# Pairs in three GpSimd instructions and six smaller moves in a two-layer gated-attention kernel

## What is computed

```
x = x + tanh(g_xattn[0]) * L0_xattn(ctx, ctx, layernorm(x), ssm_kernel, D, 8)   # (8, 256, 512)
x = x + tanh(g_ffn[0])   * L0_ffn(layernorm(x), w1, w2, w3)      # hidden 1408, ternary weights
x = x + tanh(g_xattn[1]) * L1_xattn(layernorm(x), ctx, mask)     # softmax attention on ctx
x = x + tanh(g_ffn[1])   * L1_ffn(layernorm(x), w1, w2, w3)      # hidden 2048, sign weights
# L0_xattn: kv = einsum('bhil,bhjl->bijhl', k, v); y = causal conv of kv with ssm_kernel + kv * D
#           out = einsum('bijhl,bhil->bjhl', y, q)                # 32 heads of 8
# ffn: h = silu(quant(x) @ W1.T) * (quant(x) @ W2.T); out = quant(h) @ W3.T
#      L0 quantises by row, L1 by groups of 64
```

## Time and profile before

| | us |
|---|---|
| three runs | 699.57, 700.22, 700.86 (median 700.22) |
| profiled execution | 699.74, of which span 697.6 |
| TensorE busy | 685.9 (98% of the span), granted clock 0.999 |
| VectorE / ScalarE / GpSimd busy | 587.8 / 410.1 / 273.4 |

### The profile page before, as it was taken

How to read it: one execution, slowest core, us unless ns; L and a number is a source line. 1 busy time by engine, 2 the same in 40 slices (tenths; PEclk the granted TensorE clock), 3 DMA queues, 4 the chain that set the end, 5 groups by cost and what they waited for, 6 DMA issues and landing times.

```text
span 697.6 us, 9561 instructions
## 1 busy us (share of the span) xinstructions
PE 685.9 (98%) x3172; PEld 389.6 (56%) x3172; DVE 587.8 (84%) x1066; ACT 410.1 (59%) x630; POOL 273.4 (39%) x413
## 2 busy tenths in 40 slices
PE   9999999999999999999999999999999999999997
PEld 8777777777444444567654444444444444444445
DVE  4999899899999998658958999888888888888791
ACT  3688898866579989748577544334434434434340
POOL 5779989987765654537500001111110111110000
PEclk9999999999999999999999999999999999999999
DMA  8887765553369979997040243363332333332244
GB/s 295 278 238 205 205 192 143 152 143 107 96 159 180 198 175 204 216 356 305 17 135 16 61 103 70 83 92 91 75 82 41 75 91 91 77 91 45 61 68 113
DMA packets 155376, 94.64 MB, mean 136 GB/s; under 512 B 133824, under 2 KB 134336, under 8 KB 155328
## 3 DMA queue, kind: packets, MB, share of 16 engines
q1 hardware_dynamic: 153600, 90.02, 50.6%
q0 software_dynamic: 1200, 3.93, 1.7%
q10 hardware_dynamic: 528, 0.09, 0.1%
HBM read 53.04 MB, written 8.47 MB: 88 GB/s over the span
## 4 chain that ended last, share of the span: by engine, by line
PE 73%; DVE 14%; POOL 3%; issue 3%; DMA 3%; ACT 2%; SPq 1%; POOLq 0%; ACTq 0%; DVEq 0%
PE psum L860 26%; PE psum L709 13%; PE psum L892 13%; PE psum L787 7%; PE psum L799 4%; PE psum L843 3%; PE psum L821 3%; DVE phase_space L1234 2%; DVE phase_space L1340 1%; DVE phase_space L1243 1%; DVE psum L1236 1%; DVE ln_bn L280 1%; DVE phase_space L1407 1%; PE psum L876 1%; PE psum L721 1%
## 5 line engine op out<-in xcount | busy, mean ns | idle before, releaser
L860 PE MATMUL psum<-phase_space 128*128 128x512 f16 x1024 | 224.0, 379 | 1.7 <-DMA phase_space<-phase_space 1.6
L860 PEld LDWEIGHTS psum<-phase_space 128*128 128x128 f16 x1024 | 99.9, 98 | 124.1 <-DMA phase_space<-phase_space 2.1
L709 PE MATMUL psum<-phase_space 128*128 128x288 f32 x640 | 159.2, 407 | 2.1 <-DVE phase_space L1243 1.9
L709 PEld LDWEIGHTS psum<-phase_space 128*128 128x128 f32 x640 | 120.0, 190 | 35.3 <-issue 3.2
L688 POOL DMA_DIRECT2D out<-x_sb x15 | 9.3, 620 | 303.9 <-DVE x_sb L1421 303.9
L892 PE MATMUL psum<-phase_space 128*128 128x512 f16 x480 | 105.7, 379 | 0.0
L1181 ACT ACTIVATE phase_space<-psum,b_scalars 128x512 f32<-128x512 f32 x64 | 43.5, 682 | 80.6 <-PE psum L860 78.7
L1187 ACT ACTIVATE phase_space<-phase_space,magic 128x1024 f32<-128x1024 f32 x32 | 36.4, 1147 | 77.2 <-DVE phase_space L1400 77.2
L787 PE MATMUL psum<-phase_space 128*128 128x512 bf16 (+1 forms) x384 | 79.0, 361 | 0.5 <-DVE phase_space L1282 0.5
L892 PEld LDWEIGHTS psum<-phase_space 128*128 128x128 f16 x480 | 46.9, 98 | 56.7
L1385 DVE SCALAR_TENSOR_TENSOR phase_space<-psum,b_scalars,phase_space 128x512 f32<-128x512 f32 x64 | 47.6, 747 | 25.9 <-ACT phase_space L1181 25.9
(11 more groups left out here) (122 smaller groups left out, 1039.1 us busy)
## 6 DMA issues: line engine op xcount, KB each, us to landing
phase_space<-in_L_weights SPq DMA_DIRECT2D x24, 512.0 KB, 5.8
phase_space<-in_L_weights SPq DMA_DIRECT2D x12, 704.0 KB, 7.4
phase_space<-kpad SPq DMA_DIRECT2D x14, 512.0 KB, 4.3
phase_space<-in_context_heads SPq DMA_DIRECT2D x15, 384.0 KB, 5.1
x_sb<-in_x_tiles SPq DMA_DIRECT2D x16, 256.0 KB, 4.8
phase_space<-in_context_turned SPq DMA_DIRECT2D x8, 512.0 KB, 6.1
x_between<-x_sb SPq DMA_DIRECT2D x16, 256.0 KB
x_sb<-x_between SPq DMA_DIRECT2D x16, 256.0 KB, 6.9
```

The source lines that it names most:

```text
L709: return nc.tensor.matmul(at(bank(4 * hh + lo), 0, [[64, B], [1, NP]]), toep[n % 2][:, hh, (lo - li) * P:(lo - li + 1) * P], kv[n % 2][:, ...
L860: last = nc.tensor.matmul(bank(2 * (m % 3) + w), fb_qT[n % 2][:, kk % 2, kk // 2, :], b_wT[w][:, kk // 2, c * 512:(c + 1) * 512], start=(k ...
```

## The change

Seven edits.

1. `pairs(n)` for n >= 1 writes its 24 products in three instructions of 64x8 elements, one for each distance, instead of one of 64x3x8.
2. `warm_up` issues 12 matmuls instead of 17.
3. `a_scale_x(n + 3 - NT)` of steps 13 and 14 comes behind products(n, 1) on VectorE instead of ahead of it.
4. `low_h` of tiles 0, 1 and 2 of the last FFN goes to GpSimd, with b_norm(4) between those of tiles 0 and 1; VectorE keeps tiles 3 to 15.
5. SyncE transposes x of tile 3 ahead of the rows of tile 1, instead of behind them.
6. The x side of tile 15: scale and up scales on VectorE move to the end of tile 13, ahead of fb_product(14, 0); rounding on ScalarE moves one silu ahead, and fb_deq_x ahead of fb_product(14, 1).
7. sign_b(11) moves from ScalarE's last step of the first FFN to step 0 of the attention, and c_stats(15) from step 9 to step 10.

```diff
-        NBA = 12
-        SIGN_STEP = {3: 12, 5: 13, 6: 14, 7: 15, 8: 16, 13: 17, 15: 18}
+        NBA = 11
+        SIGN_STEP = {0: 11, 3: 12, 5: 13, 6: 14, 7: 15, 8: 16, 13: 17, 15: 18}
...
-        C_STEP = {0: (4,), 1: (5,), 2: (6,), 3: (7,), 5: (8,), 6: (9, 10), 7: (11, 12), 8: (13, 14), 9: (15,)}
+        C_STEP = {0: (4,), 1: (5,), 2: (6,), 3: (7,), 5: (8,), 6: (9, 10), 7: (11, 12), 8: (13, 14), 10: (15,)}
...
                 for n in range(NT):
-                    if 2 <= n < NT - 1:
+                    if 3 <= n < NT - 1:
                         fb_turn_x(n + 1)
+                    if n == 1:
+                        fb_turn_x(3)
...
-                    nc.gpsimd.tensor_tensor(at(kv_k, E, [[NP, rows], [E, 3], [1, E]]),
-                                            at(cx_sb[k], 0, [[EX, rows], [0, 3], [1, E]]),
-                                            at(cx_sb[k], 1, [[EX, rows], [1, 3], [1, E]]), ALU.mult)
+                    for d in range(1, 4):
+                        nc.gpsimd.tensor_tensor(at(kv_k, d * E, [[NP, rows], [1, E]]),
+                                                at(cx_sb[k], 0, [[EX, rows], [1, E]]),
+                                                at(cx_sb[k], d, [[EX, rows], [1, E]]), ALU.mult)
...
+                for n in range(3):
+                    if n == 1:
+                        b_norm(4)
+                    for g in range(4):
+                        low_h(pool, nc.gpsimd, n, g)
                 for n in range(NT - 1):
-                    if n + 4 < NT:
+                    if 1 <= n < NT - 4:
                         b_norm(n + 4)
...
-                    for _ in range(17):
+                    for _ in range(12):
...
-                        if (c == 2 and 3 <= n < NT - 2) or (c == 1 and n in (2, NT - 2)):
+                        if (c == 2 and 3 <= n < NT - 2) or (c == 1 and n == 2) or (c == 0 and n == NT - 2):
                             fb_round_x(n + 1)
...
+                    products(n, 1)
                     if NT - 3 <= n < NT - 1:
                         a_scale_x(n + 3 - NT)
-                    products(n, 1)
...
                     if n == NT - 2:
-                        fb_scale_x(n + 1)
-                        fb_up_scales(n + 1)
+                        fb_deq_x(n + 1)
...
-                    for g in range(4):
-                        low_h(n, g)
+                    if n >= 3:
+                        for g in range(4):
+                            low_h(dve, nc.vector, n, g)
+                    if n == NT - 3:
+                        fb_scale_x(NT - 1)
+                        fb_up_scales(NT - 1)
```

More of the change, by code:

```diff
@@ L301, in ln_norm, with low_h @@
                                     ALU.add, ALU.mult).then_inc(s_done, 1)
+        def low_h(eng, ops, n, g):
+            eng.wait_ge(h_hi, n * 4 + g + 1)
+            if n == 3 and g == 0:
+                eng.wait_ge(h_lo, 12)
+            ops.tensor_tensor(fb_tp[n % 2][:, 1, g * 512:(g + 1) * 512], fb_t[n % 2][:, g * 512:(g + 1) * 512],
+                              fb_tp[n % 2][:, 0, g * 512:(g + 1) * 512], ALU.subtract).then_inc(h_lo, 1)
         def spread(row, groups):
@@ L1409, in deq_h @@
                                                    ).then_inc(h_u, 1)
-                def low_h(n, g):
-                    dve.wait_ge(h_hi, n * 4 + g + 1)
-                    nc.vector.tensor_tensor(fb_tp[n % 2][:, 1, g * 512:(g + 1) * 512], fb_t[n % 2][:, g * 512:(g + 1) * 512],
-                                            fb_tp[n % 2][:, 0, g * 512:(g + 1) * 512], ALU.subtract).then_inc(h_lo, 1)
                 def b_residual(n):
@@ L1575, in _ @@
                     fb_product(n, 1)
-                    if n in (2, NT - 2):
+                    if n == 2:
                         fb_deq_x(n + 1)
@@ L1618, in _ @@
                 for g in range(4):
-                    low_h(NT - 1, g)
+                    low_h(dve, nc.vector, NT - 1, g)
                 b_residual(NT - 3)
```

## The result

The changed kernel takes 693.9 us (median of six executions, 692.84 to 695.37), the kernel before 699.93 in the same comparison: a ratio of 0.9913, interval 0.9899 to 0.9926. In two later comparisons it was 692.90 (ratio 0.9899, 0.9886 to 0.9911) and 693.12 (0.9908, 0.9892 to 0.9923). It is faster by 6.0 to 6.9 us, where the forecast was 701.0 and the range ended at 694.0.

The account below looks back on a forecast made before the run. TensorE, busy 685.9 of 697.6 us, bounds the kernel; with pieces GpSimd would pace the conv stage: +3.45 us there, -2.3 behind it, net +1.15 on the profiled 699.74, lying 0.5 below the median: 701.0. Range 694 to 704.

Parts of the forecast that it names:

- Edit 1, the price of a piece: GpSimd, pairs(n): a 64x8 multiply takes 1.27 us, so three pieces add 1.0 us a step; bounds 0 and 1.0.
- The two groups: Earlier GpSimd rows: two different inputs, 2.15 ns an element and 0.18 us fixed; repeated input, 1.64 and 0.23.
- The second group's 1.07: Price in us of a 64x8 piece by the rows with repeated input (L561, L566); three take 3.1.
- The step of GpSimd: Conv stage: bare step 8.8 us, 9.8 with pieces, 10.8 with two folds, against the 10.24 TensorE needs.
- rival C: Conv stage: pieces no dearer per element than L566, step 10.1 us, GpSimd never sets the pace; 694.6 to 695.1; chance 0.33.
- The first four steps: Start of conv stage: pairs(1) ends at 19.2 us and conv(1, 0) waits for it; conv(4, 0) stays at 50.45.
- the head's gain: Edit 2: with five matmuls fewer the first conv starts 1.6 us earlier, which is spent waiting for pairs(1).
- Edit 3: End of conv stage: takes away three TensorE waits for L1243, 0.87 + 0.74 + 0.40 = 2.0 us, if nothing else is late.
- The list of waits: TensorE's waits: conv stage 0.87, 0.74, 0.40 and 0.26 us, all for VectorE; later 0.26, 0.44, 1.05 and 0.52.
- Behind the conv stage: Later waits go: edit 7 takes 0.26 and 0.44 us, edits 4 and 5 1.05, edit 6 0.52; sum -2.3 us.

Follow-up runs that it names:

- gpsimd_load: The changed kernel with one more 128x64x4 product a step on GpSimd, written to a buffer nobody reads: 702.65 us, ratio 1.004 to the kernel before.
- undo_scale: The changed kernel without edit 3, a_scale_x of steps 13 and 14 ahead of products(n, 1) again: 696.84 us, ratio 0.9957 to the kernel before.
- undo_turn: The changed kernel without edit 5, x of tile 3 transposed behind the rows of tile 1 again, edit 4 kept: 693.59 us.

## Why the prediction was wrong

**Edit 1, the price of a piece: the step that failed.** Taken at 1.27 us; 1.04 measured. The two groups of the earlier trace rows differ in three things at once (repetition, length of rows, strided or contiguous), and the prediction put it down to the first without a row that separates them. It wrote "no row proves that the repeated input is the reason" and still took the other side, because L569 looks like a piece. But L569 and L590 do not lie on one line: 256 elements in rows of 8 take 0.742 and 512 take 1.04, and the 1.26 belongs to contiguous rows. The second group's 1.07 was right to 0.03. The Trainium skill's 2.6 cycles an element (GPSIMD Engine Reference, Performance versus the Vector engine), an estimate of 1.1 us before the fixed part, fits the 1.26 of contiguous rows with a fixed part of 0.15; the 1.04 of a piece lies below it even without a fixed part. The prediction read the page rightly, and for this form the measurement decides against it.

**The step of GpSimd.** 10.8 forecast; measured 9.98 of work in a step with a pause, and 10.13 to 10.14 without one. The bare step is 8.8 + 3.12 - 2.75 = 9.17 instead of 9.8. The two folds cost 0.45 (3.57 against 3.12) and 0.33 (L596, 1.06 against 0.73) where there is a pause, and without one 0.46 each in gpsimd_load (1.18 and 1.20 against 0.72 and 0.74), which is near the forecast's 1.0 for both. So the price of the piece is all of the error: three times 0.23 is 0.7 us a step. The forecast decided at 10.24, and rival C, whose own step was 10.1, is what came. gpsimd_load, with 10.85, shows the rest of the argument to be right.

**The first four steps.** conv(1, 0) was put at 19.2, with the cheap pieces at 18.5, and started at 18.59 (18.95 and 18.73 in two other profiles). That the head's gain is spent there was right; the gain itself was 1.36 us (6.42 against 7.78) and not 1.6. What was put at nothing is the clock: the wait for pairs(1), 1.15 to 1.94 us in the changed kernel's profiles and none before, is the place where it can fall. From there conv(4, 0) starts at 48.8, where C's count gave 49.65: a block was counted at 5.04 us, its duration in a row that stands alone, but from start to start a block takes 4.87. The duration of a last matmul includes 0.17 us in which the next one would already run. The same 0.17 is missing in every wait: from 137 to 170 us the recorded waits are 2.0 us and the blocks came 2.6 later. So rival C, the one that came true, was given 694.6 to 695.1 and measured 692.9. Its gain in the conv stage was 1.5 us too small: 0.9 from this count, 0.6 from these waits. That is also why the range, which ended at C's lowest bound, missed the first median by 0.1.

**Edit 3.** The three waits for L1243, 2.0 us, were the right sum with a wrong owner: the 0.87 was L1487, held behind L566. In the forecast it made no difference, since edits 1 and 3 come together. The list of waits also left out the 0.47 and 0.54 us at 28.69 and 39.61, which are part of what the conv stage gained.

**Behind the conv stage.** -2.3 forecast and -2.3 measured: 0.71 us up to the last FFN's first matmul (355.61 - 175.32 against 350.59 - 171.01) where edit 7 had 0.70, 1.17 from there to tile 3 where edits 4 and 5 had 1.05, and 0.41 behind it where edit 6 had 0.52. Part of that is luck: the prediction left out waits of 0.50 and 0.24 us in the kernel before (188.44 and 300.06), new ones of 0.25 and 0.30 came (174.88 and 290.70), edit 5 is a double of edit 4, and edit 6 pays only while no instruction transfer falls beside it.

## What to carry to other kernels

Before a price is taken from the nearest row, list everything in which that row differs; where two causes are mixed, keep the chance of both prices, and don't put the forecast on one. Count from start to start, not by durations, and add 0.17 us here to each recorded wait. An instruction that reads two SBUF inputs on VectorE should not be allowed to queue behind a long one on GpSimd, however tiny it is; long ones on GpSimd are better cut, and whether that pays is only seen together with what is late next. And where a transfer lands just in time, look in the profile for what else is transferred beside it: a few instructions more or fewer on another engine moved that here.

## What the runs showed of the hardware

- VectorE's instructions of one element per partition with two SBUF inputs took 2.67 us (128x1) behind a GpSimd instruction of 2.75, and 0.96 (128x1) and 1.06 us (32x1) behind pieces. The Trainium skill (SBUF — State Buffer, Who interferes with whom) has this lock, and the rows agree; that a single element pays the whole of it was not expected.
- GpSimd: 64 rows of 8 in 1.04 us, 512 contiguous elements in 1.262, 32 rows of 8 in 0.742, 64 rows of 4 in 0.722; sum and product take the same in the three forms in which both were run, and a repeated input the same as a second one in the 64x3x8 form.
- A wait of TensorE of 2.20 us (undo_scale) and one of 2.72 (gpsimd_load) early in the kernel were followed by a granted clock of 0.68 and 0.59 over 4 us; one of 2.39 in undo_turn's profile was not. It cost 1.7 us.
- The same DMA transpose landed in 2.7 us in eleven profiles, in 3.3 to 4.2 in the seven in which an instruction transfer of 0.02 MB fell beside it, and in 3.2 in one without.
